# Decoder block on one core: first batch's projection and layout ahead of the others, layout by halves of the head pairs, attention output copied out by ScalarE, cross-attention values made tile by tile

## What is computed

```
x = x + attn(layernorm(x), Wq, Wk, Wv, Wo)          # 16 heads of 8, rotary, all 512 keys
x = x + xattn(layernorm(x), ctx, Wq, Wkv, Wo)       # 16 heads of 8, 32 context keys
x = x + ffn_stack(layernorm(x), ...)                # 6 layers: local attention + gated MLP

scores = einsum('bhqd,bhkd->bhqk', q, k) / sqrt(dk)
out    = einsum('bhqk,bhkd->bhqd', softmax(scores), v)
```

## Time and profile before

| | |
|---|---|
| three runs | 2062.27, 2065.89, 2071.86 us; median 2065.89 |
| profiled execution | 2066.79 us, with a span of 2065.0 us in it |
| PE busy | 1931.1 us, 94% of the span |
| DVE, ACT, POOL busy | 1519.0 us (74%), 1291.1 us (63%), 1012.1 us (49%) |
| mean granted clock of TensorE | 0.977 of full speed |
| projection, layout, softmax and values | to 262.8 us |
| cross-attention | 262.8 to 367.3 us |
| layers | 367.6 us to the end |

### The profile page before, as it was taken

The page is one execution under the profiler, slowest core; times in us unless marked ns, Lnnn a source line. Parts: engine busy times, 40 slices in busy tenths (PEclk is TensorE's granted clock), DMA queues, the critical chain, the costliest instruction groups (busy, mean ns, idle before and its releaser), DMA issues.

```text
span 2065.0 us, 46724 instructions
## 1 busy us (share of the span) xinstructions
PE 1931.1 (94%) x18988; PEld 1148.6 (56%) x18988; DVE 1519.0 (74%) x1736; ACT 1291.1 (63%) x1824; POOL 1012.1 (49%) x727
## 2 busy tenths in 40 slices
PE   5698887799999999999999999999999999999996
PEld 2121133366666666666666666666666666666663
DVE  4798555687778777877787778777877777777762
ACT  3287734466667666666676667666766676666752
POOL 7100123565556555655565656555655565555530
PEclk9699999899999999999999999999999999999998
DMA  4521010244333443334533434443444343443330
GB/s 107 87 50 25 14 39 6 84 133 105 101 101 101 124 123 101 90 104 121 132 98 97 108 104 132 110 107 90 116 117 128 92 106 100 106 112 99 104 102 19
DMA packets 105349, 195.87 MB, mean 95 GB/s; under 512 B 14096, under 2 KB 34064, under 8 KB 104880
## 3 DMA queue, kind: packets, MB, share of 16 engines
q1 hardware_dynamic: 105136, 192.88, 36.4%
HBM read 124.81 MB, written 54.79 MB: 87 GB/s over the span
## 4 chain that ended last, share of the span: by engine, by line
PE 78%; ACT 2%; issue 1%; DVE 0%; POOL 0%; DMA 0%; SPq 0%; ACTq 0%; POOLq 0%
PE ps L1358 16%; PE ps L1433 9%; PE ps L1388 9%; PE ps L1410 8%; PE ps L1367 8%; PE ps L1443 8%; PE ps L1462 6%; PE ps L1421 4%; PE ps L1398 4%; PE ps L1472 3%; PE ps L1383 2%; ACT l_v_tok L1524 1%; PE ps L1450 1%; POOL l_rot L1331 0%; ACT l_kb L1558 0%
## 5 line engine op out<-in xcount | busy, mean ns | idle before, releaser
L1331 POOL TENSOR_TENSOR l_rot<-l_rot,l_rot_s 128x1024 f32<-128x1024 f32 x192 | 455.2, 2371 | 1.0 <-DVE l_rot_s L1675 1.0
L1320 POOL COPY l_kb<-l_kb 128x512 f32<-128x512 f32 x95 | 62.9, 662 | 685.5 <-ACT l_kb L1558 685.5
L1334 POOL TENSOR_TENSOR l_rot<-l_rot,l_norms 128x1024 f32<-128x1024 f32 x192 | 365.1, 1902 | 15.1
L1663 DVE TENSOR_TENSOR l_rot<-ps,l_tab_c 128x1024 f32<-128x1024 f32 x192 | 234.9, 1224 | 165.4 <-ACT l_sq L1532 165.4
L1532 ACT ACTIVATE l_sq<-ps 128x1024 f32<-128x1024 f32 x192 | 196.8, 1025 | 206.6 <-PE ps L1358 204.0
L1675 DVE TENSOR_TENSOR l_rot_s<-ps,l_tab_s 128x512 f32<-128x512 f32 x384 | 245.5, 681 | 0.0
L1654 DVE TENSOR_REDUCE l_norms<-l_sq 128x16 f32<-128x1024 f32 x192 | 232.1, 1209 | 0.0
L1358 PE MATMUL ps<-l_wqkv,xsT 128*128 128x512 f32 x384 | 187.1, 611 | 16.4 <-ACT l_v_tok L1524 14.0
L1558 ACT ACTIVATE l_kb<-ps 64x1024 f32<-64x1024 f32 x192 | 195.7, 1019 | 1.1
L1410 PE MATMUL ps<-l_vb,l_pT 128*32 128x128 f32 x6144 | 189.4, 274 | 2.8 <-ACT l_pT L1524 1.4
L1388 PE MATMUL ps<-l_kb,l_qT 128*32 128x128 f32 x6144 | 187.6, 274 | 0.0
(11 more groups left out here) (171 smaller groups left out, 3114.3 us busy)
## 6 DMA issues: line engine op xcount, KB each, us to landing
l_vb<-v_scratch SPq DMA_DIRECT2D x336, 256.0 KB, 4.6
v_scratch<-l_v_tok SPq DMA_DIRECT2D x96, 512.0 KB, 4.9
l_vb<-v_scratch SPq DMA_DIRECT2D x48, 192.0 KB, 3.2
xsT<-xT SPq DMA_DIRECT2D x48, 135.8 KB, 2.5
stack<-scratch SPq DMA_DIRECT2D x96, 64.0 KB
l_xf<-xT SPq DMA_DIRECT2D x48, 128.0 KB, 2.4
l_wqkv_odd<-wqkv SPq DMA_DIRECT2D x9, 512.0 KB, 6.4
scratch<-parts SPq DMA_DIRECT2D x12, 256.0 KB, 2.7
```

What stands on the lines that cost most here:

```text
L1331: nc.gpsimd.tensor_tensor(rot[:, t % 2, n], rot[:, t % 2, n], rot_s[:, n], ALU.add).then_inc(added, 1)
L1334: nc.gpsimd.tensor_tensor(rot[:, t % 2, n], rot[:, t % 2, n], norms[:, t % 2, n, :, None].broadcast_to([P, HEADS, DH]), ALU.mult).then_inc ...
L1663: nc.vector.tensor_tensor(rot[:, t % 2, 1 - r], slot(name, t).rearrange("p n (h d) -> p (n h) d", d=DH), tab_c[:, 1 - r, t % TILES, None, ...
```

## The change

Two semaphores are new in the projection, so that DVE starts the cosines when q and k are made, and the sines when the rotated ones are, and a third for the layout of batch 0's second half. The orders on PE, ACT and DVE are rewritten. SP lays batch 0 out in two halves of four head pairs each (24 DMAs of 32 KB a half), then stores batch 1 and lays out its part 0. The rest of the layouts moves to other places of SP's list. `take_out` moves from DVE to ACT. In the cross-attention `values` runs for each tile of 128 queries, and ACT's copy of the result moves behind `turned`.

```diff
 sync (project_parts)
-        for b in range(2):
-            store(sp, b)
+        store(sp, 0)
+        for h in range(2):
             for part in range(3):
-                lay_out(sp, b, part)
+                lay_out_half(sp, 0, part, h)
+        store(sp, 1)
+        lay_out(sp, 1, 0)
...
+    def lay_out_half(sp, b, part, h):
+        sp.wait_ge(stored[part], 16 * (b + 1))
+        for qk, rows in enumerate((Q_ROWS, K_ROWS)):
+            for parity in range(2):
+                src = scratch[b].rearrange("(c a r) s k t -> a s r k c t", a=2, r=DK)[parity]
+                for row in rows[part]:
+                    a = parity * 64 + row * DK
+                    sp.dma_start(stack[a:a + DK, b, qk, 4 * h:4 * h + 4, :], src[part, :, qk, 4 * h:4 * h + 4])\
+                        .then_inc((laid_sems[b], second_laid)[h], 16)
...
 tensor (project_parts)
-                nc.tensor.matmul(ps[:, 3 + n, :], wat[:, w:w + P], xn[:, b % 2, :], start=True, stop=True)
+                m = nc.tensor.matmul(ps[:, 3 + n, :], wat[:, w:w + P], xn[:, b % 2, :], start=True, stop=True)
+                if n % 2:
+                    m.then_inc((qk_ready, swapped_ready)[n // 2], 1)
...
-        for s in range(STEPS):
-            if s < BATCH:
-                turn(s)
-                mean(s)
-            if 1 <= s <= BATCH:
-                variance(s - 1)
-            if s >= 2:
-                project(s - 2)
+        turn(0), mean(0), turn(1), variance(0), mean(1), project(0), variance(1), turn(2),
+        project(1), mean(2), turn(3), variance(2), mean(3), project(2), variance(3), project(3)
...
 scalar (project_parts), the whole order
-        keep_x(0), square(0), keep_x(1), square(1), inverse_deviation(0), keep_x(2), square(2),
-        inverse_deviation(1), spread_v(0), keep_x(3), inverse_deviation(2), high(0), square(3), middle(0),
-        spread_v(1), inverse_deviation(3), spread_v(2), high(1), middle(1), spread_v(3), high(2), middle(2),
-        high(3), middle(3)
+        keep_x(0), square(0), keep_x(1), inverse_deviation(0), square(1), spread_v(0), high(0),
+        inverse_deviation(1), middle(0), keep_x(2), spread_v(1), square(2), keep_x(3), inverse_deviation(2),
+        high(1), square(3), middle(1), spread_v(2), inverse_deviation(3), high(2), middle(2), spread_v(3),
+        high(3), middle(3)
...
 vector (project_parts), the whole order; "low 0" and "rest 0" are L429 and L426
-        centre 0, 1, scale 0, centre 2, scale 1, cosines 0, sines 0, add 0, centre 3, scale 2, rest 0,
-        cosines 1, low 0, sines 1, scale 3, cosines 2, sines 2, cosines 3, sines 3
+        centre 0, 1, scale 0, cosines 0, sines 0, add 0, rest 0, scale 1, low 0, cosines 1, sines 1,
+        centre 2, scale 2, centre 3, cosines 2, sines 2, scale 3, cosines 3, sines 3
...
 sync (softmax_values)
-            if half in (1, 3):
-                store(sp, 2 + half // 2)
-                lay_out(sp, 2 + half // 2, 0)
-            if half in (2, 4):
-                lay_out(sp, 1 + half // 2, 1)
-                lay_out(sp, 1 + half // 2, 2)
+            if half == 1: lay_out(sp, 1, 1), lay_out(sp, 1, 2)
+            if half == 2: store(sp, 2), lay_out(sp, 2, 0), lay_out(sp, 2, 1)
+            if half == 3: lay_out(sp, 2, 2), store(sp, 3), lay_out(sp, 3, 0)
+            if half == 4: lay_out(sp, 3, 1), lay_out(sp, 3, 2)
...
 tensor (softmax_values): PE waits for the layout at each half
-            if n == 0 and half % 2 == 0:
-                pe.wait_ge(*parts_laid[b])
+            if n == 0:
+                pe.wait_ge(*parts_laid[half])
...
 scalar (softmax_values); the same take_out leaves vector()
+        def take_out(b, g):
+            n = b * GROUPS + g
+            if n == 0:
+                act.wait_ge(parts_done, 1)
+            act.wait_ge(pv_group, (n + 1) * TILES)
+            nc.scalar.activation(outs[b][:, g, :], ps[:, 7, :], ACT.Copy).then_inc(o_read, 1)
...
+            if n >= 4 * TILES and n % (4 * TILES) == 3:
+                take_out(*divmod(n // (4 * TILES) - 1, GROUPS))
+        take_out(BATCH - 1, GROUPS - 1)
...
 cross_attention
-                def values(b):
-                    pe.wait_ge(pt_done, (b + 1) * TILES)
-                    if b >= 1:
+                def values(t):
+                    b, i = t // TILES, t % TILES
+                    pe.wait_ge(pt_done, t + 1)
+                    if i == 0 and b >= 1:
                         pe.wait_ge(o_done, b)
                     for g in range(GROUPS):
-                        m = nc.tensor.matmul(ps[:, 7, :], vb[:, b, g, :], pT[:, g, :], start=(g == 0),
-                                             stop=(g == GROUPS - 1))
+                        m = nc.tensor.matmul(ps[:, 7, i * P:(i + 1) * P], vb[:, b, g, :], pT[:, g, i * P:(i + 1) * P],
+                                             start=(g == 0), stop=(g == GROUPS - 1))
...
-                    if b_o is not None:
-                        values(b_o)
...
                     if 0 <= t - 3 < NT:
                         turn(t - 3)
+                    if 0 <= t - 4 < NT:
+                        values(t - 4)
...
 scalar (cross_attention): the copy of the result (L932) now stands behind turned(t - 3)
-                        act.wait_ge(o_ready, b_o + 1)
+                        act.wait_ge(o_ready, TILES * (b_o + 1))
```

99 lines of the change are left out of this document (62 added, 37 removed).

## The result

| | before | changed |
|---|---|---|
| median of 12 runs | 2074.91 us (2062.27 to 2080.16) | 2062.11 us (2056.95 to 2077.19) |
| profiled execution, its span | 2066.79, 2065.0 us | 2057.26, 2055.5 us |
| first maxima, round 0 | 58.41, 89.89 | 52.45, 83.72 |
| last maxima split by DVE | 230.18 | 224.29 |
| end of softmax and values (SP's first gathering of the last sums) | 263.1 | 257.7 |

The ratio is 0.9946, with a 95% interval of 0.9924 to 0.9969: 11 us faster (6 to 16), where 19.1 had been forecast; the two medians lie 12.8 us apart. The time lies above the range, which ended at 2058.5. The sum had been made against one profiled execution of 2066.8 us; against that same execution the changed kernel's profile stands 9.5 us lower, and the point was missed by 9.6.

What follows compares the result with a forecast made beforehand. PE and ACT's loop was taken to bound the rounds, with layers untouched: 2066.8 - 11.9 (start) + 1.0 (half 2) + 0.8 (take-outs) - 9.0 (cross-attention) = 2047.7 us; range 2039 to 2058.5.

Steps and rivals of the forecast that it cites:

- What bounds the kernel: Whole kernel: layers untouched, only 367 us before them in play; rounds set by PE and ACT's loop, 19.2 us a half.
- fourth rival: Rounds or projection: DVE bounds rounds, halves fall 0.9 us, or projection keeps its length; 2037 to 2042 us, chance 0.10.
- The start: Projection to first scores: first maximum at 47.5 instead of 58.4, round 0 at 78.0, 11.9 us sooner.
- its bound of 52: First maximum: latest time allowed, if one more wait for POOL comes in; the earliest was 41.8.
- a warmer PE: First maximum to round 0: PE may start maxima at the upper level, so 30.5 us instead of 31.5.
- The layout by halves: Batch 0's layout: 24 DMAs of half the bytes at 0.53 us each, 12.8 us for the first half.
- rival by the piece: Layout: a 32 KB DMA takes the 0.95 us of a 64 KB one; 2058.4 us, chance 0.08.
- Half 2: Softmax rounds: maxima's store queues behind 20 layouts, so PE waits 1 us, bounds 0 and 4.
- The take-outs: Softmax rounds: copies on ACT leave halves at 20.8 against 20.7 us; the last 12 rounds cost 0.8 us more.
- Cross-attention: Cross-attention: values per tile remove PE's 3.70 us block; 9.0 us gained, bounds 4 and 13.
- third rival: Cross-attention gains its block only, 4 us instead of 9; 2052.7 us, chance 0.13.
- 13.0 us from add 0 to add 1: Cross-attention: spacing of the first two batches' residual adds, forecast 13.0 us instead of 15.5.

Runs made afterwards that it cites:

- e1: Kernel before with only the take-outs moved from DVE to ACT; 2080.1 us in one execution.
- e7: Changed kernel with three extra unread matmuls ahead of the second batch's projection and two ahead of the fourth's; 2073.9 us in one execution.
- e3: Changed kernel with take-outs on DVE and the old cross-attention, so start and layouts alone; 2063.8 us in one execution.
- changed kernel's repeat: The changed kernel run once more, unaltered, for a second trace; 2063.3 us in one execution.
- e5: Changed kernel with, in the cross-attention, PE's values ahead of the turn and ACT's result copy ahead of `turned`; 2056.0 us in one execution.
- e10: Changed kernel with ACT's logarithm and exponential of a batch's deviation ahead of the tile's `exps` in the cross-attention; 2070.8 us in one execution.
- e6: As e5, with a batch's output, mean and variance one step sooner on PE in the cross-attention; 2072.9 us in one execution.
- e8: Changed kernel with nine extra unread matmuls ahead of the last turn of maxima; median 2063.99 us of 8 runs, ratio 0.995 to the kernel before.
- e4: Changed kernel with the projection's old orders on PE, ACT and DVE, keeping halved layout and finer semaphores; 2058.3 us in one execution.
- e11: As e10, with the projection's old orders and the take-outs back on DVE; 2048.0 us in one execution.
- e12: As e11, plus e8's filler matmuls and batch 3's last twelve layouts moved into SP's wait for the inverse; 2041.73 us, ratio 0.9841 to the kernel before.

## Why the prediction was wrong, step by step

**What bounds the kernel.** Right: the layers' own time is 1697.6 us after 1697.4, and what the stages before them gained moved them forward. That PE and ACT close the loop of the rounds, with DVE no bound, was right too; the fourth rival's first half (halves shorter by 0.9 us) is refuted by e1 and by the changed kernel's DVE, which has 2.8 of 40 us free and brings nothing.

**The start: 6.2 us instead of 11.9.** This is the larger miss. The mark that failed is the time of the first maximum, 47.5, which came at 52.45, even beyond its bound of 52. That PE would be held by the projection and not by the layout was right. The step that failed is what PE's own work was taken to cost: 3.60 us for each projection, and 1.13 and 1.02 us for the first variance and the mean behind it, which are durations at the upper level. They took 5.14 and 5.40 us (the second and fourth projection) and 2.07 and 1.91. By starts: the first projection stood at 16.41 instead of 14.9; the spacings were 9.4, 11.6 and 8.0 us instead of 9.3, 10.0 and 7.3; and the first maximum came 7.0 us behind the last projection's start instead of 6.0. Sum: 1.5 + 0.1 + 1.6 + 0.7 + 1.0 = 4.9.

Two things lengthened this work. One is the new order, which puts a wait of 3.5 and one of 2.5 us in front of two of the four projections. I had listed those waits without asking what the clock does in them; in e7, where matmuls fill them, both projections take 3.70. The other is when TensorE first rises to its upper level. The variance of the first batch (L317) in e3, and the first projection (L297) in the changed kernel's repeat:

```profile
11.31 1.13 PE L317 MATMUL ps<-work,cst 128*128 128x512 f32 x2 [0.59 <-ACT work L352]
```

```profile
16.66 5.51 PE L297 MATMUL ps<-xn,wat 128*128 128x512 f32 x8 [1.38 <-DVE xn L425]
```

The record of the granted clock, from which the windows are made, does not begin with the program: its first entry, at the upper level, is at 11.2 us in e3, just ahead of this variance, at 15.1 in the changed kernel's profile and at 20.3 in its repeat, in the middle of this projection. A window ahead of that shows 1.00 for want of a record. But in all 14 traces two f32 passes of 512 columns take 1.9 to 2.1 us ahead of the first entry and 1.0 to 1.1 behind it, so TensorE was at its lower level until then. The trace of the kernel before, from which all durations were read, has its first entry at 10.9 us, the earliest of all 14 traces (the latest is 20.8).

| trace | first entry | first projection starts | lengths of the four projections | first maximum | the same at the upper level |
|---|---|---|---|---|---|
| e3 | 11.2 | 14.67 | 3.70, 5.40, 3.70, 5.40 | 50.98 | 47.6 |
| changed | 15.1 | 16.41 | 3.70, 5.14, 3.70, 5.40 | 52.45 | 47.6 |
| e5 | 19.7 | 16.50 | 5.27, 6.61, 3.70, 3.70 | 54.24 | 47.9 |
| changed, again | 20.3 | 16.66 | 5.51, 6.72, 3.70, 3.70 | 54.77 | 48.0 |
| e10 | 20.7 | 16.56 | 5.73, 5.13, 3.70, 5.40 | 54.62 | 47.6 |
| e7 | 20.8 | 16.52 | 5.81, 3.70, 3.70, 3.70 | 51.91 | 48.0 |

The last column is an estimate: the first maximum less what the first projection starts behind e3's 14.67, less what each projection took over 3.70. It gives 47.6 to 48.0 in these six, and 47.9 in e6 and e8, where 47.5 had been forecast. So the forecast's chain of waits was right, and TensorE's clock is nearly the whole of this miss; what makes the first rise early or late stayed open. It also says what the new order itself costs against the old ones (42.9 to 43.5 in e4, e11 and e12): 4 to 5 us by its chain, and the rest of the 9 by the clock. With the old orders every projection took 3.6 to 3.9 us in e4, also with a first entry at 15.9.

From the first maximum to round 0 it took 31.3 us, not 30.5: PE stood at 0.50 through the maxima as before, and the saving of a warmer PE did not come.

**The layout by halves** was right. 24 pieces in 10.0 us (e4) are 0.42 us each, issuing included, below the 0.53 forecast. The rival by the piece, 0.95 us each, is refuted. The Trainium skill ("DMA: Bandwidth & Descriptors", Rules for kernel authors) says that below 64 KB one pays mostly overhead; for these pieces, issued back to back on one queue, the trace disagrees: half the bytes took less than half the time, and 97 GB/s moved instead of 69.

**Half 2.** The max store took 4.3 us instead of 1.8, and PE did not wait for it in the profiled execution; it did in e8, for 1.9 us. 1 us with bounds of 0 and 4 was a fair price.

**The take-outs.** Halves of 20.86 us were forecast as 20.8. The copy took 0.60 us, and ACT does not idle right behind it. The estimate of 0.73 us by the Trainium skill ("ScalarE: Activation LUTs", Rules for kernel authors), whose 0.3 us is for an ACTIVATE with its bias as a pointer operand, is above what the trace shows. The last rounds cost 0.5 us more, for 0.8 forecast.

**Cross-attention: 4.3 us instead of 9.0.** The second miss, and the third rival's size. Its condition, that DVE does most of a tile's work, is not what the runs show: e10 gains by ACT's order alone. PE's work was priced right (1.06 us for four matmuls of 128 columns; the block of 3.70 is gone). The step that failed is "13.0 us from add 0 to add 1", made by following the engines: it let ACT take the logarithm as soon as the variance was there, but ACT's list has `exps` in front of it. e10 shows 0.6 us of the missing 1.3 there, and 0.6 in the next spacing. The first add came 1.2 us sooner in the forecast and no sooner in fact: 55.8 us behind the copy of the keys after, 55.3 before. By the adds, 1.6 us of the 4.7 missing stand ahead of the first one and 3.1 between them. 0.9 of the 1.6 goes with this execution's clock: it is 0.72 in 280 to 286 us, and in the repeat, where it is 1.00 there, the first add comes 54.9 us behind the copy of the keys. The 2.6 us that are left beside these 0.9 and e10's 1.2 stay open; e5 rules the place of ACT's copy out.

Together, against the same profiled execution: start 5.7 us short, rounds 1.0 better than forecast (0.8 instead of 1.8), cross-attention 4.7 short, 0.2 in the layers, which is 9.6.

**The numbers.** The start ended beyond its poor bound and the cross-attention close to its own (4.3 us, for 4), and no case held both: the rivals were priced with one failing at a time. A gain of over 0.5% had been given 0.82; the gain came out as 0.54%, with an interval of 0.3% to 0.8%, so this is not settled. The range was also measured from a quick execution of the kernel before. Of the 14.4 us between the forecast of 2047.7 and the median of 2062.11, 8.1 are that starting point (2066.8, where the median of 12 runs is 2074.91), and 6.3 are gain that did not come. From 2074.9 the same sum would have given 2055.8, with the measured time inside a range shifted alike.

## What to carry to other kernels

When an order is rewritten so that the first item comes out sooner, look for who waits for the last item: here the maxima needed all four batches, and the new order cost 9 of the 15 us that the halved layout had won, about half of it by its chain and half by the clock. Following a chain, write for each instruction what stands before it in its own engine's list, also work of another tile, and give a matmul behind a new wait, and those at the program's start, the duration that they have at the lower clock. And where executions scatter more than the gain, compare marks within traces, one part of the change at a time.

## What the runs showed of the hardware that had not been expected

- After one and the same gap of 2.5 us in PE's work, the granted clock fell to 1.2 GHz for 14 to 41 us in six of twelve traces and stayed at 2.4 GHz in the other six. It cost 5 to 14 us, a good part of the scatter of 18 to 20 us between runs. The time of the first rise (first maximum at 51.0 to 54.8 with the same orders) and the fifth half (25.3 to 29.0 us) scatter too.
- TensorE's first rise to its upper level came between 10.9 and 20.8 us in the 14 traces, by the first entry of the clock's record. Ahead of it the f32 passes of the mean and the variance took about 1 us each (2.07 for two), behind it 0.5 (1.13 for two). The windows show a granted clock of 1.00 ahead of the record's first entry all the same, so there the durations have to be read. What decides when the rise comes stayed open.
- Eight-row layouts got faster by the byte when halved: 64 KB pieces took 1.07 us each, 32 KB pieces 0.42, most of it SP's 0.34 for issuing one. Why stayed open.
